# The portions of the FFN and the output projection issued behind the values' product of their key step

## What is computed

```python
B, S, D = 4, 2048, 256; DH = 128; H = 8; DK = 16; DFF = 1024
xn = layernorm(x)
def mha(xin, ...):                       # xin: (B, S, DH)
    q, k, v = projections, 8 heads of 16
    a = softmax(q k^T / sqrt(DK))        # full attention over 2048 keys
    return (a v) @ wo.T + bo
x1 = layernorm(xn[..., :DH] + mha(xn[..., :DH]))
xs = holt(xn)                            # exponential smoothing along the sequence
x2 = layernorm(xs[..., :DH] + mha(xs[..., :DH]))
y  = concat(x1, x2)
y  = layernorm(y + relu(y @ w_ff1.T + b_ff1) @ w_ff2.T + b_ff2)
out = x + y + (relu(xn @ W1 + b1) @ W2 + b2)      # the last term is "the FFN" of this text
```

## Time and profile before

| | us |
|---|---|
| median of three runs | 2867.13 (2863.45 to 2869.69) |
| the profiled execution | 2868.83 |
| its span | 2867.3 |
| PE busy | 2703.9 (94%) |
| ACT busy | 2117.3 (74%) |
| DVE busy | 1469.4 (51%) |
| mean granted clock of PE | 0.977 |

### The profile page before, as it was taken

How to read it: one execution, slowest core, us unless ns; L and a number is a source line. 1 busy time by engine, 2 the same in 40 slices (tenths; PEclk the granted TensorE clock), 3 DMA queues, 4 the chain that set the end, 5 groups by cost and what they waited for, 6 DMA issues and landing times.

```text
span 2867.3 us, 51522 instructions
## 1 busy us (share of the span) xinstructions
PE 2703.9 (94%) x18537; PEld 1029.6 (36%) x18537; DVE 1469.4 (51%) x3243; ACT 2117.3 (74%) x2265; POOL 176.4 (6%) x240
## 2 busy tenths in 40 slices
PE   2899999999989999999998999999999999999896
PEld 1322222235632222223572222222565222222264
DVE  7444555564554445555544454555554444435553
ACT  1599999983169999995318999999513999999720
POOL 3301010001010000000101000000011000000000
PEclk9999999999999999999999999999999999999998
DMA  3601010004010101000411011000141010100001
GB/s 134 128 9 31 9 31 9 12 5 113 30 60 9 31 11 36 9 5 19 99 45 46 21 26 31 9 9 5 49 83 41 12 31 8 31 8 12 12 18 35
DMA packets 50519, 94.89 MB, mean 33 GB/s; under 512 B 8768, under 2 KB 33344, under 8 KB 49872
## 3 DMA queue, kind: packets, MB, share of 16 engines
q1 hardware_dynamic: 39504, 65.70, 7.3%
q0 software_dynamic: 10752, 25.71, 5.7%
HBM read 57.23 MB, written 34.08 MB: 32 GB/s over the span
## 4 chain that ended last, share of the span: by engine, by line
PE 91%; DVE 4%; ACT 2%; issue 1%; DMA 1%; POOL 0%; DVEq 0%; ACTq 0%; SPq 0%; POOLq 0%
PE slot L1103 35%; PE slot L1079 19%; PE slot L1133 8%; PE slot L1142 8%; PE slot L950 7%; PE slot L964 6%; PE slot L935 2%; PE slot L1004 2%; ACT p_sb L533 1%; PE slot L1034 1%; PE slot L1043 1%; PE slot L1117 1%; PE slot L1032 1%; DVE xn L599 1%; PE slot L978 1%
## 5 line engine op out<-in xcount | busy, mean ns | idle before, releaser
L533 ACT ACTIVATE p_sb<-slot 128x1024 f32<-128x1024 f32 x2048 | 1937.7, 1028 | 168.6 <-PE slot L1079 157.1
L1103 PE MATMUL slot<-p_sb,v_sb 128*17 128x512 f32 x8192 | 1083.6, 601 | 12.8 <-ACT p_sb L533 9.9
L1079 PE MATMUL slot<-q_st,k_st 50*128 50x512 f16 x4096 | 625.2, 384 | 20.5 <-issue 11.2
L1079 PEld LDWEIGHTS slot<-q_st,k_st 50*128 50x128 f16 x4096 | 134.0, 94 | 897.6 <-ACT p_sb L533 600.6
L542 ACT ACTIVATE p_sb<-slot,con 128x512 f32<-128x512 f32 x128 | 88.0, 687 | 357.2 <-PE slot L1133 357.2
L659 DVE TENSOR_SCALAR hid_one<-slot,b_grown 128x256 f32<-128x256 f32 x256 | 123.8, 484 | 306.2 <-PE slot L950 302.7
L1103 PEld LDWEIGHTS slot<-p_sb,v_sb 128*17 128x17 f32 x8192 | 135.9, 95 | 324.1 <-ACT p_sb L533 194.4
L1133 PE MATMUL slot<-area,w_ff_sb 128*128 128x512 f32 x512 | 231.6, 612 | 5.5 <-DVE area L689 5.5
L671 DVE SCALAR_TENSOR_TENSOR second<-slot,second 128x256 f32<-128x256 f32 x64 | 27.2, 424 | 395.2 <-PE slot L964 395.2
L625 DVE RECIPROCAL rden<-den 128x256 f32<-128x256 f32 x128 | 224.4, 1753 | 7.5
L1142 PE MATMUL slot<-w_ff_sb,p_sb 128*128 128x256 f32 x1024 | 225.6, 379 | 0.0
(11 more groups left out here) (101 smaller groups left out, 1590.6 us busy)
## 6 DMA issues: line engine op xcount, KB each, us to landing
part_dram<-p_sb SPq DMA_DIRECT2D x16, 1024.0 KB, 4.6
k_st<-part_dram POOLq DMA_DIRECT2D x96, 128.0 KB, 6.2
q_st<-part_dram POOLq DMA_DIRECT2D x96, 128.0 KB, 8.2
xn<-x SPq DMA_DIRECT2D x16, 512.0 KB, 7.5
second<-x SPq DMA_DIRECT2D x32, 256.0 KB, 3.8
ffn_dram<-second SPq DMA_DIRECT2D x32, 256.0 KB, 2.0
area<-ffn_dram SPq DMA_DIRECT2D x16, 512.0 KB, 4.9
out<-area SPq DMA_DIRECT2D x16, 512.0 KB, 3.3
```

The costliest lines, as they stand in the source:

```text
L533: act.activation(p_sb[:, n % 4, :], slot[n % 3][:, :], ACT.Exp, scale=0.25 / GROW ** 2).then_inc(exp_done, 1)
L1079: mm = pe.matmul(slot[at % 3][:, k * CHUNK:(k + 1) * CHUNK], k_st[rows_, pair, kt * P:(kt + 1) * P], q_st[rows_, pair, c_ * CHUNK:(c_ + 1) ...
L1103: mm = pe.matmul(o_bank[ROW * j:ROW * j + DK + 1, :], v_sb[:, a, kt, GH * g + j, :], p_sb[:, n % 4, (j % 2) * CHUNK:(j % 2 + 1) * CHUNK], ...
```

## The change

In the loop over key steps of the attention on PE, the call of a portion (H or O) and the call of the projection (P) move from ahead of V's waits and matmuls to behind V's last matmul. No instruction is added or taken away, and no wait's value changes.

```diff
                             elif unit + 1 < UNITS2:
                                 scores(unit + 1, 0)
-                            if kt in net_kts:
-                                (second_out_part if unit % 2 else second_hidden)(b, unit // 2, net_kts.index(kt))
-                            if kt == PROJECTION_KT and unit > 0:
-                                out_projection(b, unit - 1)
                             if kt == 0:
 
                                 pe.wait_ge(o_read, u + 1)
...
                             mm.then_inc(pv_done, 1)
+                            if kt in net_kts:
+                                (second_out_part if unit % 2 else second_hidden)(b, unit // 2, net_kts.index(kt))
+                            if kt == PROJECTION_KT and unit > 0:
+                                out_projection(b, unit - 1)
```

## The result

| | before | after |
|---|---|---|
| median of three runs, us | 2867.13 | 3156.18 (3153.16 to 3160.51) |
| ratio, with its 95% interval | | 1.1008 (1.0985 to 1.1032) |
| span of the profiled execution, us | 2867.3 | 3154.6 |
| PE busy, us | 2703.9 | 2751.3 |
| ACT's idle time ahead of the exponentials, us | 168.6 | 453.3 |

What follows compares the result with a forecast made beforehand. PE was taken to set the pace, with ACT at 95%. 184.8 + 4.7 + 58.2 + 44.2 + 3.8 = 295.7 us on 2868.8 gave 3164.5, 1.7 lower for the median, rounded to 3162; range 3112 to 3225.

Steps and rivals of the forecast that it cites:

- Part 1: Within a unit, V at even key steps 2 to 14 waits 0.44 us for exponentials: 184.8 us, first units 4.7.
- Part 2: Even unit's end: V's wait for DVE's copy grows by 1.82 us to 2.08, at 32 places: 58.2 us.
- Part 3: Odd unit's end: V waits 1.58 us for DVE's copy where none was, at 28 places: 44.2 us (37 with no gap).
- Part 4: Batch ends: the shuffle comes 0.95 us later, behind DVE's two operations, at 4 places: 3.8 us.
- What I cost at nothing: Seams between blocks, DVE's chain behind a unit, stores and loads: nothing in the sum; seams 26 us either way in the range.
- The clock: Rival, chance 0.12: long unit-end waits make PE's granted clock fall, 3215 us at mildest, 3262 or 3357 in harsher cases.
- Only the unit ends: Rival, chance 0.06: V finds its exponentials done within a unit, so only unit ends cost: 106 us, 2973.
- only the exponentials: Rival, chance 0.04: only waits on exponentials cost, DVE being done with the last portion early enough: 190 us, 3057.
- not slower: Rival, chance 0.03: PE never stands for exponentials or copy, only the 0.26 us waits at 32 places change: 8 us less, 2859.

Runs made afterwards that it cites:

- the copy first: Changed kernel, but DVE copies the sums out before it reads a unit's last portion, except in a batch's last unit: 3045.7 us, ratio 1.0622.
- the last portions sooner: Kernel before, with the last two portions of each unit but a batch's first at key steps 13 and 14 instead of 14 and 15: 2857.0 us, ratio 0.9963.
- only the inner key steps: Portions and P stand behind V only at key steps 1 to 14, ahead of V at 0 and 15 as in the kernel before: 3055.1 us, ratio 1.0653.
- only the unit ends: Portions stand behind V only at key steps 0 and 15, elsewhere ahead of V as in the kernel before: 2998.3 us, ratio 1.0458.
- the even ends alone: Only the last portion of even units and the first of odd ones stand behind V, the rest as in the kernel before: 2926.5 us, ratio 1.0205.
- longer units: The even ends alone, with the second score tile computed twice at key steps 2, 4, ... 14: 3026.2 us, ratio 1.0545.
- two waits in V: Changed kernel, but V's first two heads wait only for the first exponential and the last two for the second: 3161.6 us, ratio 1.1022.

## Why the prediction was right

**Bound.** That PE sets the pace of the attention held: each us of new waits on PE appeared in the time, and nothing gave any of it back.

**Part 1** was right in mechanism and number. The limit of 2.50 us from S to V was read from two views (the earlier trace rows, an order that at the time stood only in first units), and the new trace has 2.50. The term came out at 176.0 instead of 184.8 because of the last batch: there the first exponential starts 0.43 us after its S and not 0.51, in both traces, so V waits 0.367 us and not 0.433 to 0.438. I had read the value in the first batch only.

**Part 2**: 2.06 us of wait against 2.08, 55.7 us against 58.2. Before, the mean was 0.317 and not 0.26. Here the prediction mixed two measures: 2.08 is worked out from starts, while 0.26 is the profile's idle time, which begins only at the end of the block ahead (0.83 us long, though the next can follow after 0.76). By starts the wait in the earlier trace rows is 220.61 - 219.51 - 0.76 = 0.34 us, and V, S and O are 3.05 us of work and not 3.12. That took 2 us too many. The lag behind the shuffle is not the same in every such place either: 0.13 us in three batches, 0.06 in the last. That the profile's name for this wait was wrong, and the copy the true releaser, was shown by two runs, the copy first and the last portions sooner.

**Part 3** had its mechanism right and its size wrong: 34.6 us against 44.2. The step that failed is "I take 0.25, since a wait on a semaphore stands there in either case". The semaphore `pv_done` had long been raised, and the shuffle follows the operation ahead of it without a gap. I had named zero as the other end, 37 us. The remaining 2.6 us are that the mask is loaded before the profiled end of the operation ahead, and that the shuffle with its mask took 0.72 instead of 0.75: from O to V are 193.98 - 191.44 = 2.54 us, not 2.88.

**Part 4**: some 3 us against 3.8. The shuffle comes 0.72 us later in three batches (4.49 - 3.01 - 0.76) and 0.82 in the last, and P follows 6.6 us behind it as before (6.5 in the last). The gap of 0.25 us ahead of the shuffle fell away here too.

**What I cost at nothing.** The seams kept their size: V to portion 0.986, portion to S 0.761, S to V 0.535 in the medians of all blocks. The 26 us that the range had for them weren't needed.

**The clock** was in the range and not in the sum: 17.5 us. My price for its mildest form, 1.65 us a fall, was near the 1.5 measured; that it would come at 13 of 60 places couldn't be told from the rows. The sign that I had named, a window of the attention under 0.97, missed it: with 13 falls the four windows still show 0.98 or 0.99. The other terms came out 26 us lower than forecast, and with the clock's 17.5 the forecast is 6 us from the median. So two errors cancelled in part, and that the number came this close is luck; without the clock the changed kernel would have been some 23 us below the forecast, still in the range.

**The rivals.** Only the unit ends (2973), only the exponentials (3057) and not slower (2859): each of the two chains was found at its own price by leaving out the other (+187 and +130 us, 35 of the 130 the clock's), so none of the three held. By the Trainium skill, "TensorE: Matmul & The Clock Gate", section "A second HAM failure mode: psum-queue depth-cycling", the short gaps between blocks would have made the clock swing. The runs don't agree with that rule: with waits of 0.43 us in 420 places and of at most 0.55 us at the unit ends (only the inner key steps) no fall came inside the attention.

## What to carry to other kernels

Work that stands between the making of an operand and the wait for it is cover, and its size is read as the distance from the producer's start to the consumer's earliest start, minus the work in between; here 0.44 us of it were needed and 0.76 stood there, so half a portion was enough. When a block is moved on one engine, ask which engine reads its result, and what that engine does next: DVE's order, left as it was, made 60 copies late, and turning two of its steps around took back 110 us. Where a wait is short, the name that the profile gives to its releaser should be tested by the end times of the candidates: a constant lag (0.13 us behind the shuffle in 24 of 24 such places of the first three batches, 0.06 in all 8 of the last) tells more than the name.

## What the runs showed of the hardware that I had not expected

- V's four fp32 heads leave two records each, in two rounds 0.44 us apart. When the last pair of heads is let in 0.44 us after the first, the records come in three rounds (217.45, 217.89, 218.34), and the next block follows 0.98 behind the last pair's start: splitting the wait gains nothing (1.42 us to the next block against 0.99 + 0.43 of waiting).
- Cutting a block in two, with another kind of block between the halves, costs PE some 0.11 us for a portion (2.40 us for the key step, 2.28 whole) and 0.20 for P (0.64 + 0.64 against 1.09). Whether other blocks pay the same no run here shows.
- Single waits of 1.8 to 2.2 us amid dense work can be followed by a fall of the granted clock to 0.50 for 3.4 us, at 13, 23, 3, 5 and 15 of 32 places in five runs with the same waits (the changed kernel, only the unit ends, the even ends alone, longer units, two waits in V); the waits of 1.2 us (28 places) and of 0.43 us (420) never were.
- DVE's shuffle begins with no gap after an operation that it need not wait for (0.07 us before that one's profiled end). At an even unit's end two waits stand between them, the first on the semaphore of the operation ahead, and the gap is 0.34 to 0.35 (0.27 in the last batch).
- In the batch that stands outside the loop, an exponential starts 0.43 us after its scores, and 0.51 in the three batches of the loop.
